# Attention and mixture-of-experts kernel on one core: the preparation of the first batch reordered over four accumulator banks

## The reference

```python
x = x + xattn(layernorm(x), ctx, ctx, mask, wq, wk, wv, wo)   # 16 heads of 32, 2 key/value heads
x = x + ffn(layernorm(x), ...)                                # top 2 of 8 experts, and a shared expert

def xattn(query, key, value, mask, wq, wk, wv, wo):
    Q, K, V = rope(query @ wq), rope(key @ wk), value @ wv    # split into heads
    scores = where(mask == 0, -1e9, Q @ K.T / sqrt(32))
    return (softmax(scores) @ V) @ wo
```

## Time and profile before

| what | value |
|---|---|
| median of 3 runs | 1559.9 us (1558.6 to 1561.17) |
| the profiled execution | 1558.8 us, its span 1557.0 us |
| PE busy | 1451.6 us, 93% of the span |
| DVE, ACT, POOL busy | 955.2, 910.6, 532.4 us |
| `start` (until PE turns the first probabilities) | 0 to 68.3 us |
| attention of the eight batches | 68.3 to 878 us |
| ffn phase | 878 to 1557 us |

### The profile page before, as it was taken

One profiled execution on the slowest core, in us unless ns is written; L12 is line 12 of the kernel. 1 busy time (PEld: TensorE's weight loads), 2 busy tenths in 40 slices (PEclk: granted clock), 3 DMA queues, 4 the chain that ended last, 5 costly groups with the idle time before them and its releaser, 6 DMA issues. The chain is left out here.

```text
span 1557.0 us, 37250 instructions
## 1 busy us (share of the span) xinstructions
PE 1451.6 (93%) x11434; PEld 1179.1 (76%) x11434; DVE 955.2 (61%) x2635; ACT 910.6 (58%) x2050; POOL 532.4 (34%) x665
## 2 busy tenths in 40 slices
PE   4699999999999989999989489999999999999997
PEld 3487787887887868878767367888888888888885
DVE  4487777867778778687766366666565333333332
ACT  2389888887889878888897232222221344444442
POOL 2133232331432314223222143222224455546553
PEclk9799999999999999999999789999999999999999
DMA  4234345444354443544434513222225877886652
GB/s 153 68 110 127 110 122 160 124 133 125 110 163 124 137 130 113 154 120 131 129 99 145 190 64 82 82 89 81 91 80 168 238 194 178 203 232 118 111 89 35
DMA packets 141482, 198.94 MB, mean 128 GB/s; under 512 B 34903, under 2 KB 72543, under 8 KB 141282
## 3 DMA queue, kind: packets, MB, share of 16 engines
q1 hardware_dynamic: 120738, 157.81, 33.3%
q0 software_dynamic: 17952, 33.64, 11.6%
q10 hardware_dynamic: 2592, 4.98, 0.9%
HBM read 97.10 MB, written 69.35 MB: 107 GB/s over the span
## 5 line engine op out<-in xcount | busy, mean ns | idle before, releaser
L896 DVE CUSTOM_DVE_ANT_0 a_probs<-a_psum,a_bias 128x512 f32<-128x512 f32 x512 | 348.6, 686 | 168.4 <-PE a_psum L711 156.8
L528 ACT ACTIVATE a_probs<-a_probs,a_low 128x512 f32<-128x512 f32 x512 | 369.0, 721 | 105.4 <-DVE a_low L896 101.2
L623 PE MATMUL a_psum<-a_ident,a_probs 128*128 128x128 f32 x2048 | 318.2, 278 | 19.3 <-DVE a_xT_lo L843 6.2
L623 PEld LDWEIGHTS a_psum<-a_ident,a_probs 128*128 128x128 f32 x2048 | 242.7, 141 | 90.7 <-issue 38.3
L711 PE MATMUL a_psum<-a_kT,a_q_stack 128*128 128x512 f32 x512 | 249.5, 488 | 9.1 <-DMA a_q_stack<-a_qT_lo 5.6
L534 ACT ACTIVATE a_probsT<-a_psum 128x512 f32<-128x512 f32 x400 | 234.2, 586 | 12.1 <-issue 6.6
L1246 POOL DMA_INDIRECT out<-b_y,b_pairs_sb x71 | 113.2, 1594 | 147.2 <-DMA out<-b_y,b_pairs_sb 87.2
L730 PE MATMUL a_psum<-a_probsT,a_v 128*32 128x128 f32 x4096 | 139.6, 277 | 7.4 <-ACT a_probsT L534 4.7
L1689 DVE SCALAR_TENSOR_TENSOR b_v_hidden<-b_v_hidden,b_psum 128x256 f32<-128x256 f32 x71 | 29.9, 421 | 165.3 <-ACT b_v_hidden L1348 165.3
L730 PEld LDWEIGHTS a_psum<-a_probsT,a_v 128*32 128x32 f32 x4096 | 105.1, 110 | 30.0 <-issue 17.4
L446 POOL CAST a_w_hi<-a_w_raw 128x256 fp32r<-128x256 f32 x96 | 38.6, 402 | 259.4 <-DMA a_w_raw<-in_L_ffn_Wd 126.3
(11 more groups left out here) (206 smaller groups left out, 3156.6 us busy)
## 6 DMA issues: line engine op xcount, KB each, us to landing
b_w<-w_halves SPq DMA_DIRECT2D x16, 1536.0 KB
a_q_stack<-a_qT_hi SPq DMA_DIRECT2D x256, 64.0 KB, 2.0
a_q_stack<-a_qT_lo SPq DMA_DIRECT2D x256, 64.0 KB, 2.0
w_halves<-a_w_hi SPq DMA_DIRECT2D x96, 128.0 KB, 1.8
w_halves<-a_w_lo SPq DMA_DIRECT2D x96, 128.0 KB, 1.9
a_x_in<-in_x SPq DMA_DIRECT2D x32, 256.0 KB, 2.9
a_ctx_in<-in_ctx SPq DMA_DIRECT2D x32, 256.0 KB, 3.9
a_x_res<-in_x SPq DMA_DIRECT2D x32, 256.0 KB, 3.0
```

Source lines behind the costliest of these rows:

```text
L528: nc.scalar.activation(probs[:, h % 2, t], probs[:, h % 2, t], ACT.Exp, bias=low[:, h % H, t:t + 1], scale=-1.0, accum_out=total[:, h // G ...
L623: last = nc.tensor.transpose(out[:, P * i:P * (i + 1)], src(i), identity[:])
L896: nc.vector.tensor_tensor_reduce(probs[:, h % 2, t], psum[:, t % 2], bias[:, t], 1.0, HUGE, ALU.add, ALU.min, low[:, h % H, t:t + 1]).then ...
```

## The change

- The ring of four banks is used in `start` too: each turning operation and kv product waits only for the one four places before it.
- q's four products of `start` go to four banks (`product_bank`), so none waits for a rotation.
- The order in `start` on PE: kv, turn_ctx of the next tile, q, turn_x of the next tile, turn_k of the tile before. ACT and DVE follow; DVE normalises tiles 0 and 1 ahead of everything else, and takes xT_lo of the next tile ahead of the rotation of q.
- Loads: SP has ident, pick, x and ctx 0, wq in four chunks, x and ctx 1, the other tiles, and wo last, into a half of `q` instead of `probs`. ACT's queue issues wk, wv, rope_k, rope_q and the mask. PE's first instruction waits for ident and pick alone.
- wq is rounded and split in four chunks, and q's first product waits chunk by chunk. wo is split on POOL at the beginning of `first`, by two operations over 128 x 2048; the first rotation of q in `first` waits for it.
- The placing rules of `first`, `middle` and `last` become tables (`PE_AT`, `ACT_AT`, `DVE_AT`). Written out, PE's order in them is the same as before. On DVE the `normalise` of tile 0 and of tile 2 each move ahead of a copy out of PSUM (steps 3 and 19), `normalise` 1 and 3 ahead of `scale` (att), turned_k 0 ahead of moments 3, and add_residual 0 ahead of `scale`. On ACT, turned_ctx 1 and 3 move behind one exponential. On POOL finish_k comes one head earlier and ahead of finish_q. In `end` all three `weighted` now precede the spreading of 1/sum (before, the third came behind it).

```diff
-                        for dst, src in ((ident, k["ident"]), (pick_raw, k["pick"]), (rope_q, k["rope_q"]), (rope_k, k["rope_k"])):
-                            sp.dma_start(dst[:], src).then_inc(s["const_in"], 16)
+                        for dst, src in ((ident, k["ident"]), (pick_raw, k["pick"])):
+                            sp.dma_start(dst[:], src).then_inc(s["ident_in"], 16)
                         load_x(b, 0)
                         load_ctx(b, 0)
-                        sp.dma_start(probs[:, 0], wq.rearrange("(c p) n -> p c n", p=P)).then_inc(s["wq_in"], 16)
-                        sp.dma_start(wkv[:, :, 0:KV], wk.rearrange("(c p) n -> p c n", p=P)).then_inc(s["kv_in"], 16)
-                        sp.dma_start(wkv[:, :, KV:2 * KV], wv.rearrange("(c p) n -> p c n", p=P)).then_inc(s["kv_in"], 16)
+                        for c in range(DC):
+                            sp.dma_start(probs[:, 0, c], wq[P * c:P * (c + 1)]).then_inc(wq_in[c // 2], 16)
                         load_x(b, 1)
                         load_ctx(b, 1)
-                        sp.dma_start(probsT[:, 0:TT].bitcast(I32), mask.rearrange("a b (t p) k -> p (a b t) k", p=P)).then_inc(s["mask_in"], 16)
-                        sp.dma_start(probs[:, 1], wo.rearrange("(c p) n -> p c n", p=P)).then_inc(s["wo_in"], 16)
                         for t in range(2, TT):
                             load_x(b, t)
                             load_ctx(b, t)
+                        sp.dma_start(q[:, par], wo.rearrange("(c p) n -> p c n", p=P)).then_inc(s["wo_in"], 16)
...
+                def split_wo(par):
+                    pool.wait_ge(s["wo_in"], 16)
+                    alone(pool, s["passed"])
+                    nc.gpsimd.tensor_copy(wo_hi[:], q[:, 1 - par]).then_inc(s["wo_rounded"], 1)
+                    pool.wait_ge(s["wo_rounded"], 1)
+                    nc.gpsimd.tensor_tensor(wo_lo[:], q[:, 1 - par], wo_hi[:].bitcast(F32), ALU.subtract).then_inc(s["wo_split"], 1)
...
                     if part == "start":
-                        at = orders[part].index((kind, i)) - 1
+                        at = start.index((kind, i)) - len(RING)
                         if at >= 0:
-                            wait_emptied(b, *orders[part][at], 0)
-                        return psum[:, TURN]
+                            wait_emptied(b, *start[at], 0)
...
                     if part == "start":
                         turn_x(part, b, 0)
                         turn_ctx(part, b, 0)
-                        pe.wait_ge(s["weights_split"], 1)
+                        pe.wait_ge(s["kv_in"], 32)
                         for t in range(TT):
                             project_kv(part, b, t)
+                            if t + 1 < TT:
+                                turn_ctx(part, b, t + 1)
                             for c in range(DC):
                                 project_q(part, b, t, c)
                             if t + 1 < TT:
                                 turn_x(part, b, t + 1)
-                                turn_ctx(part, b, t + 1)
-                            turn_k(part, b, t)
+                            if t > 0:
+                                turn_k(part, b, t - 1)
+                        turn_k(part, b, TT - 1)
                         turn_q(part, b, par, HG)
...
                     if part == "start":
-                        dve.wait_ge(s["const_in"], 64)
+                        dve.wait_ge(s["ident_in"], 32)
                         nc.vector.tensor_copy(ident_r[:], ident[:]).then_inc(s["consts_ready"], 1)
                         nc.vector.tensor_copy(pick[:], pick_raw[:]).then_inc(s["consts_ready"], 1)
-                        stats_of(b, 0)
-                        moments_of(b, 0)
-                        normalise(b, 0)
-                        dve.wait_ge(s["wq_rounded"], 1)
-                        nc.vector.tensor_tensor(wq_lo[:], probs[:, 0], wq_hi[:].bitcast(F32), ALU.subtract).then_inc(s["weights_split"], 1)
+                        for t in range(2):
+                            stats_of(b, t)
+                            moments_of(b, t)
+                            normalise(b, t)
                         x_low(part, b, 0)
-                        stats_of(b, 1)
-                        moments_of(b, 1)
-                        normalise(b, 1)
+                        for c in range(DC):
+                            dve.wait_ge(s["wq_rounded"], c + 1)
+                            nc.vector.tensor_tensor(wq_lo[:, c], probs[:, 0, c], wq_hi[:, c].bitcast(F32), ALU.subtract).then_inc(s["weights_split"], 1)
+                        dve.wait_ge(s["const_in"], 32)
                         for t in range(TT):
                             projected_kv(part, b, par, t)
                             if t == 0:
-                                dve.wait_ge(s["wo_rounded"], 1)
-                                nc.vector.tensor_tensor(wo_lo[:], probs[:, 1], wo_hi[:].bitcast(F32), ALU.subtract).then_inc(s["weights_split"], 1)
                                 dve.wait_ge(s["mask_in"], 16)
...
-                            projected_q(b, par, t)
                             if t + 1 < TT:
                                 x_low(part, b, t + 1)
-                            turned_k(part, b, par, t)
+                            projected_q(part, b, par, t)
+                            if t > 0:
+                                turned_k(part, b, par, t - 1)
```

More of the change, by code:

```diff
@@ L179, in group_done, with stages @@
+        def stages(part, table, at):
+            return [(kind, i) for kind, i in table.get(at, ()) if there(part, kind, i)]
         def group_done(part, h):
@@ L182, in group_done @@
             return None if part == "first" and g < 0 else g
-        def turns(part):
-            return [turn_at(part, h, pos) for h in range(H) for pos in range(4) if turn_at(part, h, pos)]
         start = [("xT", 0), ("ctxT", 0)]
@@ L190, in attention_phase @@
             if t + 1 < TT:
-                start += [("xT", t + 1), ("ctxT", t + 1)]
-            start += [("kT", t)]
+                start += [("ctxT", t + 1), ("xT", t + 1)]
+            if t > 0:
+                start += [("kT", t - 1)]
+        start += [("kT", TT - 1)]
         start += [("qT", HG), ("qT", HG + 1)]
-        orders = {"start": start, "first": turns("first"), "middle": turns("middle"), "last": turns("last"),
-                  "end": [("inverse", -1), ("spread", -1)]}
         before = {"middle": "middle", "last": "middle", "end": "last"}
@@ L231, in in_bank_before @@
                     at, back = at + len(line), back + 1
-                    if part not in before:
-                        return None
+                    if part == "first":
+                        return [e for e in start if ring_bank("start", *e) == RING[at % len(RING)]][-1], back
                     part = before[part]
@@ L675, in project_q @@
                         pe.wait_ge(s["xT_split"], upto(b, "xT", t))
-                        if t > 0:
+                        if t > 0 and part != "start":
                             pe.wait_ge(s["q_rotated"], upto(b, "q", t - 1))
@@ L679, in project_q @@
                             pe.wait_ge(s["q_rotated"], upto(b, "q", -1))
-                    last = product(psum[:, PRODUCT], xT_hi[:, P * c:P * (c + 1)], xT_lo[:, P * c:P * (c + 1)], wq_hi, wq_lo, c)
+                    if t == 0 and part == "start":
+                        pe.wait_ge(s["weights_split"], c + 1)
+                    last = product(psum[:, product_bank(part, t)], xT_hi[:, P * c:P * (c + 1)], xT_lo[:, P * c:P * (c + 1)], wq_hi, wq_lo, c)
                     if c == DC - 1:
@@ L758, in beside @@
                             spread_inverse(part, b, i)
-                    if pos == 1 and weighted_at(part, h):
-                        weighted(b, par, *weighted_at(part, h))
-                    products()
+                        if kind == "out":
+                            for t, tiles, after in OUT_STEPS:
+                                if (GH * i + GH - 1) * TT + after == u:
+                                    weighted(b, par, i, t, tiles)
+                        if kind == "q":
+                            project_q(part, b, i // DC, i % DC)
+                        if kind == "wo":
+                            project_out(part, b, par, i // DC, i % DC)
                 def body(part, b, par):
@@ L927, in add_residual, with beside @@
                     nc.vector.tensor_tensor(x_res[:, t % 2], psum[:, bank], x_res[:, t % 2], ALU.add).then_inc(s["x2_ready"], 1)
+                def beside(part, b, par, u):
+                    for kind, i in stages(part, DVE_AT, u):
+                        if kind == "stats":
+                            stats_of(b, i)
+                        if kind == "moments":
+                            moments_of(b, i)
+                        if kind == "xn":
+                            normalise(b, i)
+                        if kind == "x_low":
```

(15 more changed lines are left out.)

292 lines of the change are left out of this document (113 added, 179 removed), and 9 rows, old and new, of the table PE_AT.

## The result

| | time, us | ratio to before, 95% interval |
|---|---|---|
| before, 5 runs | 1561.17 (1558.6 to 1563.86) | |
| after, 5 runs | 1550.35 (1550.15 to 1552.61) | 0.9936 [0.9922, 0.9951] |

The account below looks back on a forecast made before the run. PE was taken to bound the kernel, with half of `start` spent waiting and passed on to the end one for one. Gains 1.35 + 11.4 + 2 - 0.65 = 14.1 us gave 1545.5 us, range 1541 to 1552.

Parts of the forecast that it names:

- The head: `start` until q's first product ends: x 1 lands at 15.1, q ends at 23.8 instead of 25.16; 1.35 us gained.
- that rival: In `start`, all of ACT's 1.57 MB goes ahead of x 1, landing at 16.6; up to 1548.5 us; chance 0.14.
- The steps: `start`, from the end of q's first product to turn_q: 20.0 us against 31.36, 11.4 us gained.
- The rival of the low clock in `start`: The clock stays low for q's products in `start`; 5.8 us given back, 1551 us; chance 0.13.
- no gain: DVE's chain through POOL sets `start` steps of 9 to 10 us as before; gain 0 to 3, 1558; chance 0.05.
- wo's split: In `first`, POOL's two 2048-column operations take at most 10 us and are covered; cost 0, bounds 0 to 1 us.
- The tables: Attention batches: earlier normalise saves 2 of PE's 3.3 us of waits; +2 us (-2 to 4.5).
- the rival of 21 us: Steady loop: five DVE operations put back hold PE 3 us a batch over 7 batches; 1568 us; chance 0.04.
- a sign of being wrong: Steady loop: a batch taking over 0.5 us more than before would show the prediction wrong.
- `end`: In `end`, scale starts at 860.4 instead of 859.77; -0.65 us (-1.3 to 0).

Follow-up runs that it names:

- d_mask: The kernel after with the mask issued on SP behind x 1 and ctx 1, not on ACT's queue; 1546.43 us, ratio 0.9921.
- h_all: The kernel after with `start`'s ring shifted one bank, wo split at `start`'s end, spreading before the third `weighted`, mask on SP; 1544.34 us, ratio 0.9887.
- e_onebank: The kernel after with all turning operations and kv products of `start` in one bank again; 1571.06 us, ratio 1.0066.
- a_ring: The kernel after with the ring of `start` shifted by one bank; 1550.51 us, ratio 0.9940.
- c_end: The kernel after with the spreading matmul of `end` ahead of the third `weighted` again; 1549.68 us, ratio 0.9942.
- j_after: The kernel after run once more, unchanged; 1553.85 us, ratio 0.9942.
- b_wo: The kernel after with POOL's split of wo at the end of `start`, not in `first`; 1548.92 us, ratio 0.9940.
- i_xfirst: The kernel after with `start`'s ring shifted, wo split earlier, old `end` order, mask on SP, and x 1 and ctx 1 ahead of wq; 1548.99 us, ratio 0.9904.
- g_dve: The kernel before with only after's DVE order of normalise, add_residual, scale and evacuation in first, middle and last; 1561.59 us, ratio 1.0000.

## Why the prediction was right, point by point

**The head.** Right in its mechanism: x 1 sets it, then statistics, normalise, xT_lo and a quarter of wq's split. The 3.9 us of that chain took 3.88 (13.60 to 17.48). The size was off: x 1 landed at 13.6, not 15.1, and the gain was 2.4, not 1.35. q's product then took 5.26 us and not 4.81, since none of its matmuls ran at the faster pace. The step that failed is the base of the sum, "If no more of ACT's queue goes ahead than came ahead before, x 1 lands at 13.6": without the mask in the second queue it landed at 10.8 and 11.8 (d_mask, h_all). Over those microseconds the transfers moved more than before, 365 instead of 240 GB/s in 6 to 8 us; that this comes of the two queues, and not of the other order of loads, wasn't tested apart. The mask does stand in the way, 1.5 to 2.9 us against the 3.0 reckoned, of which I had taken half. So the second queue did hold x 1 up, as that rival had it, but from an earlier landing. The Trainium skill's rule on sharing between queues, cited in the prediction, agrees with this in that the mask in ACT's queue was served along with SP's; the landing of 16.6 worked out with it did not come, and equal shares aren't shown.

**The steps.** From q's end to turn_q 20.15 us against 20.0. Within it two errors cancelled. The first step took 6.05 (5.73 or 5.74 in the seven such profiles in which the matmuls were up to pace by then), not 5.2, because turn_x 2 needs normalise 2, which I had put into the second step; and of the 0.6 us that I had added for the clock only 0.3 came, 20.15 against 19.8. The wait I named (kv's bank) did not come, PE waits for normalise (0.59, 0.89) and xT_lo (0.42). Both are DVE's chain, so that "DVE sets this step, at 6.0" held (6.10). The clock stayed up, as chosen. The rival of the low clock in `start` and that of "no gain" fell. The first was priced too high besides: it took 4.81 for a product at the low clock, the first one's time, where the two behind the gaps took 3.69 and 3.91 in before. e_onebank shows that in the new order there is no gain without the ring: one bank turns it into a loss.

**wo's split.** Wrong. "In `first` DVE mostly reads PSUM" overlooked the normalise, an operation of 512 columns from SBUF to SBUF, which the new order puts beside POOL's cast. The cast held it for 1.3 us (1.5 in a_ring, c_end, e_onebank and j_after), until 0.28 or 0.29 behind its own end, and b_wo, h_all and i_xfirst, without the cast beside it, have it at 0.55. The 6.5 us of the two operations together lay under my 10. The Trainium skill states it ("SBUF — State Buffer", section "Who interferes with whom"): an operation such as `tensor_scalar` may use the port pair that VectorE and GpSimd share, and the one that starts first keeps it for the whole instruction. The traces agree: DVE's own subtraction had held POOL's cast the other way round in before, and DVE's operations on PSUM beside POOL's subtraction stay at 0.67 to 0.69.

**A bank I didn't check.** I wrote out the ring in `start` and not its passage into `first`: the second turning of probabilities takes the bank of the last q turning. Wait 2.15 us. It cost after 1.0 us, with the granted clock at 0.50, and under 0.1 in the three profiles with the same wait in which the clock had risen; the held normalise cost 1.3. Together the lead fell from 13.6 to 11.3, where I had counted nothing.

**The tables.** +2 predicted, none found. g_dve's batches do not show the 0.55 us each that the wait took, though g_dve has the new order of DVE's normalise, residual and scale alone, not turned_k 0 nor ACT's and POOL's order. The six batches take 606.1 us in before and 605.3 in g_dve, and 604.3 to 609.8 in the ten profiles with all of the tables, so a loss of a few microseconds isn't excluded; the rival of 21 us is. Per batch, on average, j_after is 0.6 us over before, past the 0.5 that the prediction gave as a sign of being wrong, and after 0.2; with this scatter the sign was set too fine. "Some comes back as a wait for ACT's exponentials" is borne out for the 1.3 us of the weight loads only. This was the weakest term, a wait total taken for a gain.

**`end`.** -0.65 predicted, -0.41 measured up to scale (c_end). Between the 509th `lowest` and the end of the attention after lost 1.5 in all; PE's granted clock was 1.00 in the last 16 us of before (862 to 878) and 0.90 in the same work of after (853 to 869). The other 1.1 us are not the order's doing: c_end, with the old one, lost 1.6 there and had 0.93 in 853 to 869. The single profile of before was quick in this place.

**The sum.** Up to the end of the attention the profiles have 9.2 (j_after 8.8) and the forecast 14.1. Term by term: `start` 13.6 instead of 12.75 (+0.9); `first` -2.3 instead of 0; the tables 0 instead of +2; the rest of the loop -0.5, not foreseen; `end` -1.5 instead of -0.65 (-0.9). That is 4.8 less, 9.3. The medians gave 10.8 here and 7.6 in the runs of j_after (1561.44 to 1553.85); the 9.2 lies between them. The count was not exact: of the three terms behind `start`, two were wrong, and `first` was not counted at all. That the time fell within the range is luck in part: it lies 1.65 us from the upper end, and the same kernel's six runs in j_after lie above it, 1552.07 to 1554.77. Above all, the ffn phase alone scatters by 4.6 us, over a third of the range's width.

Open: what of the split's 1.3 to 1.5 us is left at the end of the attention, since a_ring, with the split in place, reached the same 869.55 as b_wo; and what lets the clock rise or fall some microseconds earlier or later in `first` at the same point of the program. It was worth up to 1.6 us between profiles, in both directions (g_dve had 0.59 in 80 to 84 us where before had 1.00, lost 1.6 and was 0.5 ahead at the 509th `lowest`).

## What to carry to other kernels

A single shared bank makes every reader a wait for every writer, and what it costs can grow when work is moved forward into it (here `start` became 6.1 us longer than before); lay out the ring and its passage into the next stage together, entry by entry. Before moving work to GpSimd, look for VectorE operations beside it that go from SBUF to SBUF, not only at the cover behind it. A wait total on the bounding engine is an upper bound for a gain: ask which wait ends last once it is gone, and check the time of a single batch, not the label of another wait. Run the changed kernel a second time: an effect is known only against what its own profiles scatter by.

## What was not expected of the hardware

Two queues moved 337, 365 and 407 GB/s in 4 to 6, 6 to 8 and 8 to 10 us (after), one queue 259, 240 and 344 in the same stretches (before), where the order of the loads differs too. A GpSimd cast of 1.89 us held a VectorE operation of 0.55 us until 0.29 us after its own end. GpSimd's cast of 2048 columns takes 1.89, its subtraction with two SBUF operands 4.50 to 4.62, twice VectorE's 2.29. One wait of 2.15 us cost TensorE's chain 1.0 us at the lower clock and under 0.1 once it had risen.

The column of the granted clock doesn't tell it all. Two stretches of the kernel after, q's first product and its second:

```profile
17.50:22.70 5.20, 5.20 (x12) 4.02 (x13) 3.24 (x8) 0.00 (x0) 2.08 (x4) 1.00 0.00 0
25.20:28.00 2.80, 2.80 (x12) 2.11 (x12) 2.01 (x6) 0.43 (x1) 1.65 (x2) 1.00 0.81 254
```

Both have 12 matmuls of the same shape and 1.00 in the column, but one takes 5.2 us and the other 2.8: at the start of the work the matmuls' own durations (0.63, then 0.39) have to be read too. q's first product, and kv 0 and the turns ahead of it, therefore have another price than their like in later steps, and not a fixed one: the pace changed behind the third to the twelfth matmul, and the product took 3.63 to 5.26 us in the ten profiles of the new order.
